# Orders of all engines with fewer changes between the matmul kinds of TensorE, and a gate transpose from a padded tile

## The chip, the cores and the metric

The kernel runs on one core of one Trainium2 chip. The metric is the device time of one execution in microseconds (us), lower is better.

## The reference

128 sequences (B) of S = 128 positions with D = 256 features, and a context of the same shape, go through four layers. All arithmetic is in float32.

```python
# layer 0, for every sequence; 16 heads of 16
z  = mha(x, x, Wq1, Wk1, Wv1, causal=True);  x1 = layernorm(x + z)
z  = mha(x1, ctx, Wq2, Wk2, Wv2);            x2 = layernorm(x1 + z)
x  = layernorm(x2 + relu(x2 @ fc1.T + b) @ fc2.T + b)
# inside mha: lengths = sum(energy[:, :, 0, :] != 0); key columns beyond the length get -inf
# layer 1: gate of width 4
nX, nF = layernorm(ctx), layernorm(x)
h  = gelu(attention(nF, nX, nX) @ fc1_w.T + fc1_b)      # 4 values a position
cr = h @ fc2_w.T + fc2_b;   nc = layernorm(cr)
x  = nF + gamma2 * (cr + gamma1 * attention(nc, nc, nc))
# layer 2
x  = x + softmax(x @ ctx.T) @ ctx
# layer 3: the mixer, 8 heads of 32, then a scan over the positions
y  = x + mha(layernorm(x), layernorm(ctx)) @ W_o.T + b_o
u  = (layernorm(y) @ W_in.T + b_in) @ Bmat
s_t = silu(s_{t-1} @ A.T) + u_t;   out = y + s @ Cmat + mod
```

## The kernel before

The sequences are worked on in 64 groups (g) of two (`G = 2`, line 25). The kernel has a prelude (weights, constants), a main phase over the groups, and a last phase for the scan over the 128 positions. The change is in the main phase.

**Software pipeline.** The work on a group is cut into some hundred steps per engine, each in one of ten units (`self_in`, `self_att`, `ctx_in`, `ctx_att`, `ffn`, `pair`, `real`, `mix_in`, `mix_att`, `mix_out`). `PROGRAM` (line 132) writes out by hand the order of steps on each engine. An entry such as `pair.yT@5` means: in round i, run step `yT` of unit `pair` for group i - 5. The number after the @ is the lag. `drive` (line 242) runs one order for rounds 0 to 69 and leaves out groups that don't exist; on SP the full rounds are a loop, on the other engines they are unrolled. Each step waits, by semaphores that count finished steps, for what it reads and for the buffer it writes (`Steps`, `Ring`). `BANKS` gives each product of TensorE one of eight PSUM banks; a bank is free when the step that read its last content is done. TensorE's 109 entries are the longest order in time.

**Steps of TensorE.** They differ in which part of the 128 x 128 array they use:
- over the whole array: `turned` (four transposes of 128 columns, L652), the transposes of probabilities `turn` (L730) and of outputs `back` (L777), projections (eight matmuls of 256 columns, L660 and L668), a bfloat16 causal tile of 512 columns (L679), and the pair steps (L831 to L909). A float32 matmul that is no transpose shows as two MATMUL records;
- in row strips: `scores.br` (L700) for sequence b and strip r, and `scores_mix` (L717), whose operands lie in 32 partitions each;
- in column strips: `values.br` (L764, the mixer's L759) and `e0` (L810), whose stationary operand has 32 columns and whose output is 32 partitions. A step of self and ctx values has one product in each of the four strips; a mixer's step r has its four products in two strips, `(DH * r + a) % 4 * 32`, the strips 0 and 1 for even r, 2 and 3 for odd r.

**The gate.** `gelu` writes four values a position into `y5`, whose fifth column is 1 (it carries the bias). `yT` transposes it on TensorE (L874), ScalarE copies five partitions of the result (L1051), and `cross` multiplies them by `w_cross` (L882):

```python
y5 = sb("y5", [128, G, 5])
last = nc.tensor.transpose(t[0:5, b * S:(b + 1) * S], y5[:, b, :], ident[:])
```

**The load of x.** `x` is held in one buffer. `load_self` (L594) waits until the group before has been transposed by TensorE (`xT`) and read by VectorE (`amax`, L1204):

```python
waits_apart(sp, prep, *latest(self_in["pe"].before("xT", g), self_in["dve"].before("amax", g)))
sp.dma_start(nat["X"][:], x_g[g]).then_inc(x_in.sem, 16)
```

**VectorE** takes the maxima of the scores (L1144), subtracts them (L1155), sums the mixer's rows (L1166) and does the statistics of the norms; **ScalarE** does exponentials (L978) and copies PSUM to SBUF (L968, L988, L1003); **GpSimd** does gains, biases and residual sums; **SP** issues all loads and stores.

## Time and profile before

| | |
|---|---|
| median of 3 runs | 4374.66 us (4370.78 to 4374.66) |
| the profiled execution's own time | 4371.99 us |
| its span, first to last instruction | 4370.2 us |
| instructions | 112146 |
| busy: TensorE, VectorE, ScalarE, GpSimd | 94%, 80%, 73%, 66% |
| granted TensorE clock, mean | 0.986 |

PE is TensorE's matmul, PEld its load of the stationary operand, which runs beside it; DVE is VectorE, ACT ScalarE, POOL GpSimd, SP the engine that issues DMAs. An engine's busy time counts overlapping instructions once. Matmuls are pipelined: one starts long before the end of the one before, so what a matmul costs in a stream is the distance between two starts and not its duration. A line of the timeline gathers equal neighbours (x8 is eight instructions).

### The profile page before, as it was taken

What the parts mean: (1) busy time and instruction counts of PE and PEld (TensorE: products, weight loads), DVE (VectorE), ACT (ScalarE), POOL (GpSimd) and SP (SyncE); (2) the same over time, 40 slices, a digit from 0 to 9 for tenths busy, and PEclk for the clock granted to TensorE, in tenths of its full rate; (3) what the DMA queues carried; (4) which work ended last, traced back from release to release, by engine and by line L of the source; (5) the groups of instructions that cost most, each with busy time, mean ns of one, the idle gap of its engine ahead of it and who ended that gap; (6) DMA issues with size and microseconds to landing.
All of it is one profiled execution on the core that took longest, in us unless ns stands there. A gap on an engine that the chain in (4) does not pass through costs nothing. (4 is left out here: it accounts for less than half of the span.)

```text
span 4370.2 us, 112146 instructions
## 1 busy us (share of the span) xinstructions
...
## 2 busy tenths in 40 slices
...
DMA packets 127586, 159.99 MB, mean 37 GB/s; under 512 B 23925, under 2 KB 114362, under 8 KB 122618
## 3 DMA queue, kind: packets, MB, share of 16 engines
...
q14 instruction: 242, 1.98, 0.2%
...
## 5 line engine op out<-in xcount | busy, mean ns | idle before, releaser
L988 ACT ACTIVATE probT<-bank 128x512 f32<-128x512 f32 x1280 | 741.4, 597 | 340.3 <-PE bank L730 337.0
L1144 DVE TENSOR_REDUCE mx<-bank 128x4 f32<-128x512 f32 x1280 | 834.4, 681 | 138.1 <-PE bank L700 104.2
L1155 DVE TENSOR_TENSOR prob<-bank,mx 128x512 f32<-128x512 f32 x1280 | 857.5, 683 | 40.1 <-PE bank L730 15.4
L978 ACT ACTIVATE prob<-prob 128x512 f32<-128x512 f32 x1280 | 783.5, 638 | 29.3 <-DVE prob L1155 28.0
L968 ACT ACTIVATE turned<-bank 128x512 f32<-128x512 f32 x896 | 531.8, 602 | 346.5 <-PE bank L652 192.7
L730 PE MATMUL bank<-ident,prob 128*128 128x128 f32 x5120 | 750.3, 280 | 31.8 <-POOL prob L1480 20.9
L730 PEld LDWEIGHTS bank<-ident,prob 128*128 128x128 f32 x5120 | 569.3, 142 | 126.9 <-issue 92.3
L660 PE MATMUL bank<-turned,shared 128*128 128x256 f32 x2560 | 606.0, 384 | 2.3 <-ACT turned L968 2.3
L660 PEld LDWEIGHTS bank<-turned,shared 128*128 128x128 f32 x2560 | 473.9, 191 | 81.7 <-issue 23.2
L1469 POOL TENSOR_SCALAR shared<-turned,half_of 128x512 f32<-128x512 f32 x256 | 397.9, 1565 | 200.7 <-ACT turned L968 200.7
L1390 POOL TENSOR_TENSOR rs_ln<-ve_ln,half 128x2 f32<-128x2 f32 x320 | 225.8, 705 | 333.1 <-DVE ve_ln L1133 333.1
L700 PE MATMUL bank<-shared,turned 32*128 32x256 f32 x4096 | 373.8, 403 | 11.4 <-POOL shared L1469 2.1
L668 PE MATMUL bank<-shared,turned 128*128 128x256 f32 x1536 | 369.9, 384 | 0.2 <-ACT probT L988 0.2
L1404 POOL TENSOR_TENSOR X<-X,row_ln_g 128x512 f32<-128x512 f32 x192 | 245.6, 1279 | 174.2 <-ACT X L1038 167.1
L1480 POOL TENSOR_TENSOR prob<-prob,inv 128x512 f32<-128x512 f32 x256 | 266.5, 1042 | 127.6 <-DVE inv L1171 127.6
L764 PE MATMUL bank<-probT,shared 128*32 128x128 f32 x8192 | 316.6, 278 | 9.1
L700 PEld LDWEIGHTS bank<-shared,turned 32*128 32x128 f32 x4096 | 264.2, 186 | 71.7 <-issue 65.7
L668 PEld LDWEIGHTS bank<-shared,turned 128*128 128x128 f32 x1536 | 277.0, 190 | 38.4 <-ACT probT L988 0.6
L764 PEld LDWEIGHTS bank<-probT,shared 128*32 128x32 f32 x8192 | 196.6, 109 | 119.1 <-issue 118.4
L1410 POOL TENSOR_TENSOR X<-X,row_ln_b 128x512 f32<-128x512 f32 x192 | 244.3, 1273 | 15.1
L844 PE MATMUL bank<-turned 128*128 128x128 f32 x1536 | 210.4, 280 | 3.0 <-ACT turned L968 2.9
L844 PEld LDWEIGHTS bank<-turned 128*128 128x128 f32 x1536 | 187.2, 192 | 11.7 <-ACT turned L968 4.1
...
## 6 DMA issues: line engine op xcount, KB each, us to landing
shared<-in_x SPq DMA_DIRECT2D x128, 256.0 KB, 3.5
CB<-in_ctx SPq DMA_DIRECT2D x64, 256.0 KB, 3.2
CC<-in_ctx SPq DMA_DIRECT2D x64, 256.0 KB, 2.7
mod<-mod_rows SPq DMA_DIRECT2D x64, 256.0 KB, 3.5
residual<-X SPq DMA_DIRECT2D x64, 256.0 KB, 2.2
...
```

Source lines behind the costliest of these rows:

```text
L660: last = nc.tensor.matmul(t[:, m * W:(m + 1) * W], w[:, a, m * 128:(m + 1) * 128], src[:, a, :], start=(a == 0), stop=(a == DH - 1))
L668: last = nc.tensor.matmul(t[:, b * D:(b + 1) * D], src[:, a, b * S:(b + 1) * S], w[:, a, :], start=(a == 0), stop=(a == DH - 1))
L700: last = nc.tensor.matmul(t[:, a * W:(a + 1) * W], QT[p][rows_, a, b * S:(b + 1) * S], KEYS[p][rows_, a, :, b * S:(b + 1) * S], start=(p ! ...
L730: last = nc.tensor.transpose(t[:, h * 128:(h + 1) * 128], src[:, h, :], ident[:])
L764: last = nc.tensor.matmul(t[k * 32:(k + 1) * 32, r * 128:(r + 1) * 128], VP[p][:, b, 4 * r + k, :], src[:, k, :], start=True, stop=True)
L844: last = nc.tensor.matmul(t[:, b * S:(b + 1) * S], qT[:, a, b * S:(b + 1) * S], kT[:, a, b * S:(b + 1) * S], start=(a == 0), stop=(a == DH ...
L968: nc.scalar.activation(dst, banks.of(f"{unit}.{name}")[:, 0:n], ACT.Copy).then_inc(*st["act"].mark(name))
L978: nc.scalar.activation(flat(t), flat(t), ACT.Exp, scale=SCALE[p]).then_inc(*st["act"].mark(f"exp.{b}{r}"))
L988: nc.scalar.activation(flat(t), banks.of(f"{att}.turn.{b}{r}")[:, :], ACT.Copy).then_inc(*st["act"].mark(f"probT.{b}{r}"))
L1144: nc.vector.tensor_reduce(m[:], banks.of(f"{att}.tile.{b}{r}")[:, :].rearrange("p (h t) -> p h t", h=4), AX, ALU.max)\
L1155: nc.vector.tensor_tensor(t[:], banks.of(f"{att}.tile.{b}{r}")[:, :].rearrange("p (h t) -> p h t", h=4), maxes.of(f"{att}.max.{b}{r}")[:]. ...
L1469: last = nc.gpsimd.tensor_scalar(KEYS[p][:, :, c, :], KT[p][:], half_of[:, c:c + 1], None, ALU.mult)
```

## The change

The orders of TensorE, ScalarE, VectorE, GpSimd and SP are written anew. The steps are the same, with some at another lag (`self_in.e0` at 1 and not 2, `self_in.amax` at 2 and not 1, `real.ccT` at 5 and not 4, `ctx_att.copies` at 3, `pair.load` at 4 and so on). TensorE's new order has longer runs of `values` and `scores` steps next to each other. All bank numbers are new. `y5` gets 128 columns for each sequence, all set to 1 in the prelude, and is transposed whole, into 128 partitions of the bank; ScalarE still copies five.

```diff
     "pe": """
-        self_in.e0@2 mix_att.scores.00@6 ctx_att.turn.10@4 ctx_att.values.00@4 ctx_att.values.01@4 ctx_att.turn.12@4
-        ctx_att.turn.11@4 pair.yT@5 ctx_att.values.03@4 ctx_att.turn.13@4 pair.cross@5 self_att.causal.02@2
-        ctx_att.values.02@4 ctx_att.values.12@4 self_att.causal.00@2 self_att.causal.03@2 ctx_att.values.10@4
-        ctx_in.x1T@3 self_att.causal.01@2 ctx_att.back.0@4 self_att.scores.01@2 self_att.scores.02@2
-        self_att.scores.00@2 self_att.scores.03@2 ctx_att.values.11@4 ctx_att.values.13@4 mix_att.turn.03@6
-        mix_in.k@5 ctx_att.back.1@4 mix_att.turn.02@6 ctx_in.q@3 pair.ncT@5 self_att.causal.10@2 mix_att.values.02@6
-        mix_att.values.03@6 mix_att.turn.00@6 self_in.len@2 pair.sc2@5 self_att.turn.01@2 mix_att.turn.01@6
-        self_att.causal.11@2 self_att.causal.12@2 mix_att.values.00@6 self_att.scores.10@2 self_att.scores.11@2
-        self_att.scores.12@2 pair.pT2@5 mix_att.values.01@6 ctx_in.cT@3 pair.av@5 mix_in.v@5 ffn.x2T@4 ctx_in.k@3
-        ffn.fc1@4 real.x4T@5 self_att.turn.03@2 ctx_in.e0@3 self_att.turn.00@2 real.screal@5 ffn.fc2@4 mix_out.o@6
-        real.pTreal@5 self_in.xT@1 self_att.turn.02@2 real.av@5 self_att.causal.13@2 self_att.scores.13@2
-        ctx_att.scores.02@3 ctx_att.scores.00@3 ctx_att.scores.03@3 ctx_att.scores.01@3 self_att.values.01@2
-        self_att.values.00@2 self_att.values.03@2 self_att.values.02@2 self_att.turn.10@2 ctx_in.v@3 self_in.q@1
-        ctx_in.len@3 self_att.turn.12@2 self_att.turn.11@2 self_att.turn.13@2 self_in.v@1 self_att.back.0@2
-        ctx_att.turn.00@3 ctx_att.turn.01@3 self_att.values.10@2 self_att.values.12@2 self_att.values.13@2
-        self_att.values.11@2 ctx_att.scores.10@3 ctx_att.scores.12@3 ctx_att.scores.13@3 ctx_att.scores.11@3
-        self_in.k@1 pair.CT@4 real.ccT@4 mix_out.h6T@6 pair.FT@4 self_att.back.1@2 ctx_att.turn.03@3 real.h5T@5
-        pair.sc1@4 ctx_att.turn.02@3 pair.vx@4 mix_in.q@5 pair.pT1@4 mix_out.u@6 pair.av1@4
+        mix_att.scores.00@6 ctx_att.turn.12@4 ctx_att.values.01@4 ctx_att.values.03@4 ctx_att.values.00@4
+        ctx_att.values.02@4 pair.yT@5 ctx_att.turn.10@4 ctx_att.turn.11@4 pair.cross@5 self_att.causal.02@2
+        ctx_in.x1T@3 real.ccT@5 ctx_att.turn.13@4 mix_in.k@5 ctx_att.back.0@4 self_att.causal.00@2
+        ctx_att.values.10@4 ctx_att.values.13@4 ctx_att.values.12@4 ctx_att.values.11@4 self_att.causal.03@2
+        self_att.causal.01@2 self_att.scores.01@2 self_att.scores.03@2 self_att.scores.02@2 self_att.scores.00@2
+        mix_att.turn.03@6 ctx_att.back.1@4 ctx_in.q@3 mix_att.turn.02@6 pair.ncT@5 self_in.len@2 mix_att.turn.00@6
+        self_in.xT@1 pair.sc2@5 self_att.causal.11@2 self_att.causal.10@2 self_att.causal.12@2 mix_att.turn.01@6
+        self_att.scores.10@2 self_att.scores.12@2 self_att.scores.11@2 mix_att.values.00@6 mix_att.values.02@6
+        mix_att.values.01@6 mix_att.values.03@6 pair.pT2@5 self_att.turn.01@2 ctx_in.cT@3 pair.av@5 mix_in.v@5
+        self_att.turn.00@2 ffn.x2T@4 ctx_in.k@3 ffn.fc1@4 real.x4T@5 ctx_in.e0@3 self_att.turn.03@2
+        self_att.causal.13@2 real.screal@5 ffn.fc2@4 mix_out.o@6 real.pTreal@5 self_att.turn.12@2 self_att.turn.02@2
+        real.av@5 ctx_in.len@3 self_att.scores.13@2 ctx_att.scores.03@3 ctx_att.scores.00@3 ctx_att.scores.01@3
+        ctx_att.scores.02@3 self_att.values.00@2 self_att.values.02@2 self_att.values.03@2 self_att.values.01@2
+        self_in.q@1 self_att.turn.11@2 self_att.turn.10@2 ctx_in.v@3 self_att.turn.13@2 self_att.back.0@2
+        self_in.v@1 ctx_att.turn.00@3 ctx_att.turn.01@3 self_att.values.12@2 self_att.values.13@2
+        self_att.values.10@2 self_att.values.11@2 ctx_att.scores.10@3 ctx_att.scores.13@3 ctx_att.scores.11@3
+        ctx_att.scores.12@3 pair.CT@4 self_in.k@1 mix_out.h6T@6 pair.FT@4 ctx_att.turn.03@3 real.h5T@5
+        self_att.back.1@2 pair.sc1@4 mix_in.q@5 ctx_att.turn.02@3 pair.vx@4 pair.pT1@4 mix_out.u@6 pair.av1@4
+        self_in.e0@1
     """,
...
     "dve": """
-        self_att.ln1ve@3 self_in.nz@2 self_in.count@2 mix_att.max.03@6 mix_att.max.00@6 mix_att.max.02@6
-        mix_att.centre.03@6 mix_att.centre.02@6 mix_att.max.01@6 mix_att.centre.00@6 mix_att.centre.01@6
-        mix_att.sum.03@6 self_in.spread@2 mix_att.recip.03@6 pair.lnNstats@5 pair.lnNaggr@5 ctx_in.amax@3
-        pair.lnNve@5 mix_att.sum.02@6 ctx_att.recip.0@4 mix_att.recip.02@6 ctx_att.norm.0@4 mix_att.sum.00@6
...
-        ctx_att.centre.10@3 ctx_att.centre.12@3 pair.NXT@4 self_in.amax@1 ctx_att.centre.11@3 ctx_att.max.13@3
...
+        mix_att.centre.03@6 mix_att.max.02@6 mix_att.max.01@6 mix_att.centre.02@6 mix_att.centre.01@6
+        mix_att.sum.03@6 mix_att.recip.03@6 pair.lnNstats@5 mix_att.centre.00@6 pair.lnNaggr@5 self_in.spread@2
+        pair.lnNve@5 mix_att.sum.02@6 ctx_att.recip.0@4 mix_att.recip.02@6 mix_att.sum.00@6 ctx_att.norm.0@4
+        mix_in.k@5 self_in.amax@2 mix_att.recip.00@6 self_att.max.01@2 mix_att.sum.01@6 ctx_att.recip.1@4
...
+        pair.a4@4 self_in.count@1 mix_att.max.03@5 mix_att.max.00@5
     """,
...
     "sp": """
-        mix_out.load@6 mix_out.store@6 mix_out.store_u@6 ctx_in.load@2 self_att.load@1 self_in.load@0 pair.load@3
+        pair.load@4 ctx_in.load@2 self_att.load@2 mix_out.load@5 mix_out.store@6 self_in.load@0 mix_out.store_u@6
     """,
...
-        y5 = sb("y5", [128, G, 5])
+        y5 = sb("y5", [128, G, 128])
...
-                        last = nc.tensor.transpose(t[0:5, b * S:(b + 1) * S], y5[:, b, :], ident[:])
+                        last = nc.tensor.transpose(t[:, b * S:(b + 1) * S], y5[:, b, :], ident[:])
```

## Rows read from the trace of the kernel before

**Rows 1.** Windows: stretch, length, busy PE, PEld, DVE, ACT, POOL, PE clock, DMA, GB/s.

```profile
249.00:3986.00 3737.00, 3699.43 (x34368) 3044.37 (x34548) 3173.46 (x8726) 2931.84 (x6162) 2644.68 (x2928) 1.00 0.09 28
```

**Rows 2.** Line 874, the gate's transpose: duration min/median/max ns, first and last start.

```profile
L874 PE MATMUL bank<-ident,y x128: 272/273/275, 249.0 to 4163.1; 128*5 128x128 f32 x128
```

**Rows 3.** Waits, PE's costliest, 1000 to 3000 us: us in total, times, longest.

```profile
PE bank L717 <- DVE mv_ln L1126: 0.8, 2, 0.5
```

**Rows 4.** Timeline, PE, 2052 to 2057: start us, length us, line, count.

```profile
2052.36 1.17 PE L717 MATMUL bank<-keys,turned 32*128 32x128 f32 x32
2053.46 0.66 PE L730 MATMUL bank<-ident,prob 128*128 128x128 f32 x4
2054.05 0.64 PE L764 MATMUL bank<-probT,shared 128*32 128x128 f32 x16
2054.62 1.09 PE L730 MATMUL bank<-ident,prob 128*128 128x128 f32 x8
2055.61 0.38 PE L874 MATMUL bank<-ident,y 128*5 128x128 f32 x2
2055.93 0.42 PE L764 MATMUL bank<-probT,shared 128*32 128x128 f32 x8
2056.28 0.66 PE L730 MATMUL bank<-ident,prob 128*128 128x128 f32 x4
2056.78 1.03 PE L882 MATMUL bank<-w_cross,y5T 128*128 128x256 f32 x4
```

**Rows 5.** Timeline, PE, 2021 to 2045.

```profile
2021.64 1.89 PE L668 MATMUL bank<-shared,turned 128*128 128x256 f32 x8
2023.37 1.89 PE L668 MATMUL bank<-w_o,turned 128*128 128x256 f32 x8
...
2040.02 1.29 PE L700 MATMUL bank<-shared,turned 32*128 32x256 f32 x16
2041.25 1.99 PE L660 MATMUL bank<-turned,shared 128*128 128x256 f32 x8
2043.08 0.60 PE L652 MATMUL bank<-ident,HC 128*128 128x128 f32 x4
2043.52 0.60 PE L652 MATMUL bank<-ident,CC 128*128 128x128 f32 x4
2044.12 0.66 PE L652 MATMUL bank<-ident,H 128*128 128x128 f32 x4
```

**Rows 6.** Timeline, PE, 2005 to 2010, with the mixer's values (L759).

```profile
2005.74 0.66 PE L759 MATMUL bank<-probT,vp 128*32 128x128 f32 x16
2006.33 0.66 PE L730 MATMUL bank<-ident,prob 128*128 128x128 f32 x4
...
2009.33 0.63 PE L759 MATMUL bank<-probT,vp 128*32 128x128 f32 x8
2009.89 1.15 PE L700 MATMUL bank<-shared,turned 32*128 32x256 f32 x12
```

**Rows 7.** Groups by form, 1000 to 3000 us: busy us, mean ns, idle before.

```profile
L730 PEld LDWEIGHTS bank<-ident,prob 128*128 128x128 f32 x2564 | 282.9, 141 | 46.0 <-issue 31.7 <-ACT probT L988 6.2 <-DVE mx L1144 0.4
...
L874 PEld LDWEIGHTS bank<-ident,y 128*5 128x5 f32 x64 | 3.0, 85 | 5.2 <-ACT probT L988 1.5
```

**Rows 8.** Timeline, SP: issues of loads, start us, length us.

```profile
2053.76 0.37 SPq L600 DMA_DIRECT2D shared<-in_x  x1
2054.50 1.57 SPq L594 DMA_DIRECT2D shared<-in_x  x1
```

**Rows 9.** Timeline, DVE, 2053 to 2063.

```profile
2053.66 1.89 DVE L1144 TENSOR_REDUCE mx<-bank 128x4 f32<-128x512 f32 x3 [0.49 <-PE bank L717]
...
2062.42 0.68 DVE L1166 TENSOR_REDUCE den<-prob 128x4 f32<-128x512 f32 x1
```

**Rows 10.** DMA issues, KB each, us to landing: 2020 to 2045, then 1990 to 2120.

```profile
CC<-in_ctx SPq DMA_DIRECT2D x1, 256.0 KB, 3.8
...
shared<-in_x SPq DMA_DIRECT2D x6, 256.0 KB, 4.3
```

More of the change, by code:

```diff
@@ L177 @@
-        self_att.centre.10@2 pair.sa@5 self_att.max.12@2 self_att.max.11@2 self_in.keep@2 ctx_in.q0@3 self_in.vp@2
-        ffn.relu@4 ctx_in.nz@3 self_att.centre.11@2 real.mxreal@5 real.nmreal@5 self_att.centre.12@2 ffn.sum@4
-        real.rsreal@5 ffn.ln3stats@4 ffn.ln3aggr@4 ffn.ln3ve@4 ctx_in.count@3 mix_out.res@6 mix_out.ln6stats@6
-        real.x5@5 ctx_att.max.00@3 ctx_att.max.01@3 self_att.max.13@2 real.ln5stats@5 ctx_att.centre.00@3
-        mix_out.ln6aggr@6 ctx_in.spread@3 self_att.centre.13@2 pair.lnFstats@4 pair.lnFaggr@4 ctx_att.max.03@3
@@ new lines @@
+        self_att.centre.01@2 ctx_att.norm.1@4 self_att.max.00@2 self_att.max.02@2 mix_att.recip.01@6
+        self_att.centre.00@2 ctx_att.ln2stats@4 self_in.valid@2 ctx_att.ln2aggr@4 pair.mx2@5 ctx_att.ln2ve@4
+        self_in.keep@2 pair.nm2@5 ctx_in.amax@3 ctx_in.keep@3 self_att.max.03@2 self_att.centre.03@2
+        self_att.centre.02@2 pair.rs2@5 self_att.max.11@2 self_att.max.12@2 pair.sa@5 self_att.centre.12@2
+        self_att.max.10@2 ctx_in.q0@3 self_att.centre.11@2 self_in.vp@2 ffn.relu@4 self_att.centre.10@2 ctx_in.nz@3
@@ new lines @@
+        ctx_in.count@3 real.mxreal@5 real.nmreal@5 ffn.sum@4 ctx_in.spread@3 ffn.ln3stats@4 real.rsreal@5
+        ffn.ln3aggr@4 ffn.ln3ve@4 mix_out.res@6 mix_out.ln6stats@6 mix_out.ln6aggr@6 ctx_in.valid@3 mix_out.ln6ve@6
+        real.x5@5 self_att.max.13@2 ctx_att.max.00@3 ctx_att.max.01@3 ctx_att.centre.00@3 self_att.centre.13@2
+        real.ln5stats@5 pair.lnFstats@4 ctx_att.centre.01@3 pair.lnFaggr@4 pair.lnFve@4 real.ln5aggr@5
+        pair.lnCstats@4 ctx_att.max.02@3 pair.lnCaggr@4 self_att.recip.0@2 real.ln5ve@5 self_in.q0@1 pair.lnCve@4
@@ L188 @@
     """,
     "pool": """
-        self_att.add@3 real.x5b@6 ctx_att.copies@4 self_att.ln1pow@3 ffn.copies@4 self_att.ln1nmr@3 ffn.biased@4
-        self_att.keep@3 self_att.ln1gain@3 self_att.ln1@3 mix_att.part.03@6 pair.lnNpow@5 pair.lnNnmr@5
-        mix_att.part.02@6 pair.lnNgain@5 pair.lnN@5 mix_att.part.00@6 ctx_att.add@4 mix_att.part.01@6
-        ctx_att.ln2pow@4 ctx_att.ln2nmr@4 ctx_in.mask@3 ctx_att.ln2gain@4 ctx_att.ln2@4 pair.skip@5 pair.gam2@5
-        pair.x4@5 ctx_in.keys@3 ffn.x2b@4 ffn.ln3pow@4 ffn.ln3nmr@4 ffn.ln3gain@4 ffn.ln3@4 pair.lnFpow@4
@@ L195 @@
-        mix_out.ln6pow@6 pair.lnFnmr@4 mix_out.ln6nmr@6 pair.lnCpow@4 pair.lnCnmr@4 pair.lnFgain@4 real.ln5pow@5
-        real.ln5nmr@5 pair.lnF@4 mix_out.mod@6 self_in.keys@1
+        self_in.keys@2 mix_att.part.03@6 pair.lnNpow@5 pair.lnNnmr@5 mix_att.part.02@6 pair.lnNgain@5 pair.lnN@5
+        mix_att.part.00@6 ctx_att.add@4 mix_att.part.01@6 ctx_att.ln2pow@4 ctx_att.ln2nmr@4 ctx_in.mask@3
+        ctx_att.ln2gain@4 ctx_att.ln2@4 pair.skip@5 pair.gam2@5 pair.x4@5 ffn.x2b@4 ctx_in.keys@3 ffn.ln3pow@4
@@ L209 @@
-    ctx_att.tile.01:0 ctx_att.tile.02:7 ctx_att.tile.03:4 ctx_att.turn.00:2 ctx_att.turn.01:1 ctx_att.turn.02:5
-    ctx_att.turn.03:0 ctx_att.back.0:6 ctx_att.tile.10:0 ctx_att.tile.11:1 ctx_att.tile.12:6 ctx_att.tile.13:3
-    ctx_att.turn.10:4 ctx_att.turn.11:2 ctx_att.turn.12:5 ctx_att.turn.13:5 ctx_att.back.1:4 ffn.x2T:1 ffn.fc1:6
-    ffn.fc2:0 pair.CT:7 pair.FT:4 pair.vx:4 pair.sc1:2 pair.pT1:5 pair.av1:3 pair.yT:4 pair.cross:4 pair.ncT:1
-    pair.sc2:1 pair.pT2:1 pair.av:1 real.x4T:1 real.ccT:2 real.screal:1 real.pTreal:5 real.av:2 real.h5T:7
```

64 lines of the change are left out of this document (34 added, 30 removed).

## Prediction

> **What bounds the kernel now.** I read first which engine is busiest, and where. The table by windows says that from 249 to 3986 us TensorE is busy 3699 of 3737 us at a granted clock of 1.00, VectorE 3173, ScalarE 2932, GpSimd 2645 [rows 1]. The gate's transpose, once in each round of the pipeline, first runs at 249.0 and last at 4163.1 us, 64 rounds [rows 2]; 3914 us over 63 intervals is 62.1 us a round, and near 62.4 in the full stretch. The waits say who is late there: in 2000 us TensorE waits 0.8 us in its costliest group [rows 3]; the idle time of the others is theirs to spend. So TensorE's own order sets the pace. A microsecond taken from one round is taken from about 63: some 60 rounds are full (3737 / 62.4), and I count the partly filled ones at both ends as 3 more.
>
> A busy TensorE is not one at its peak, so the next view is its timeline, read by the starts of neighbouring lines. The steps come in three kinds: over the whole array (F), in column strips (C: values, e0), in row strips (R: scores). The difference of two starts shows a price wherever the kind changes:
> - Without a change, a step of four transposes takes 0.44 us (2043.08 to 2043.52), 0.11 for each; a projection of eight records 1.73 (2021.64 to 2023.37), so 0.22 for 256 columns, and as much for a causal tile; a C step of eight records 0.22, since 16 of them take 0.57 and 8 take 0.35 [rows 4, 5].
> - F to C: the two transposes at 2055.61 take 0.32 in place of 0.22, so 0.10 is lost. Within the stay, 16 matmuls take 0.57 in place of 0.44, 0.13 lost. Back in F, the four at 2056.28 take 0.50, 0.06 lost. One stay in C costs 0.29 us; I book 0.14 on entering C and 0.15 on returning to F [rows 4].
> - A projection after R takes 1.83 in place of 1.73 [rows 5].
>
> **The change, part by part.**
> *Orders.* Going once round each order, with the wrap, gives 29 changes of kind before and 20 after. Runs of C go from 12 to 7, of R from 5 to 5, of F from 12 to 8. Of the returns to F, one before and one after begins with a causal tile and one with a projection; these cancel. The others begin with transposes: ten before, six after. So 5 x 0.14 + 4 x 0.15 = 1.30 us a round go. One R run that followed C now follows F; I take both entries as equal, the nearest rows being 0.10 for F to C and 0.12 for C to R (2009.33 to 2009.89 is 0.56 for what takes 0.44 in itself) [rows 4, 6].
>
> *The mixer's values.* A step of these uses two of the four strips for four turns of 0.11 us. Before, steps 02 and 03, of unlike strips, took 0.59 together, and a single step 0.56 [rows 6]; 00 and 01 stood alone. Less 0.13 for each of three stays that is 1.32 us. After, one stay holds 00, 02, 01, 03. If nothing overlaps, 4 x 0.44 = 1.76; if both pairs do, 0.88. Only the middle pair are neighbours of unlike strips, so I take the middle, 1.32: no change, with -0.44 and +0.44 as ends.
>
> *The padded gate tile.* The transpose now loads 128 columns, not 5: 141 ns and not 85 [rows 7]. Transposes start every 0.11 us whichever they load, so it is hidden; uncovered twice a round it would be 0.1 us. It now follows a C run directly, and the return to F is counted above. The one memset of the larger tile stands outside the loop. Zero.
>
> *Moved waits.* VectorE, ScalarE and GpSimd keep their instructions, with 9.4, 13 and 18 us free in a round [rows 1]. ScalarE and GpSimd are given new places, but what TensorE needs of them keeps a microsecond or so of other matmuls between, as before: I take zero, and the rival on waits holds the rest. One distance shrinks much. The load of x for a round waits until VectorE's amax has read the last one (single buffer). amax moves from the end of VectorE's order to its first fifth (@1 to @2), TensorE's transpose of x from the middle to the first third, both now in the same round. Before, x is issued at 2054.50 [rows 8] and is wanted a half round later. After: VectorE's first maximum starts 1.30 us after the mixer's scores start (2053.66 against 2052.36), and the same sequence up to its third sum ends 9.4 us on, at 2063.1 [rows 4, 9]. It loses one reduction and gains the keys and amax, +0.6: amax ends 11.4 us after the scores. TensorE, from the same start to the transpose of x: 1.10 for the scores, 12 x 0.44 for transposes, 0.22 for the gate's, 0.87 cross, 2 x 1.73, 4 x 0.22 causal, 0.1 length, 8 x 0.22 values, 1.23 for a run of scores with its way out, 0.29 for each of two stays in C and 0.2 for the other changes: 15.7 us. That leaves 4.3 us less some 0.1 for semaphores, 4.2, for a load. Lone and crowded loads land in 3.8 and 4.3 us [rows 10], and SP takes up to 0.7 us from one issue to the next [rows 8], so 3.8 to 5.0 are needed: a stall of 0 to 0.8 us a round. I take 0.2, what the middle of both gives (4.4). SP's other loads are then issued behind it or behind real.av, with half a round or more before their use: zero. Behind a late x TensorE's whole order queues, from a quarter of the round on; next in it are the gate's second scores and the self tiles, for which VectorE and ScalarE wait.
>
> *Sum.* 1.30 - 0.20 = 1.10 us a round, x 63 = 69 us. The profiled execution took 4371.99 us, 1.8 over its span and 2.7 under the median 4374.66: 4303 in its terms, **4305 us** in the median's, 1.6% less.
>
> A rule to weigh: the rows show 0.10 us lost on entering C and 0.15 in all on returning [rows 4]. The Trainium skill (TensorEngine Tiling (Array Packing), Tiling Modes) says that a change of tiling mode drains the TensorE, which this agrees with. Its page TensorE: Matmul & The Clock Gate (Single matmul latency, Back-to-back issue gap) prices an isolated warm matmul at (398+N)/2.4 ns against N/2.4 + 2.5 in a stream; an estimate from that page is 163 ns a drain, 9 x 0.163 x 63 = 92 us in place of 82, and 4295 us in all. The trace's prices hold in the sum.
>
> **The rivals.**
> - *Half given back.* x comes 0.5 to 1.2 us late, or new waits of that size stand at other tight places. For it: 4.2 us against 3.8 to 5.0. Against: where TensorE itself lags in the steps before, the gap is wider. 0.1 to 0.8 us a round remain: 4324 to 4368. Chance 0.20.
> - *Slower.* The same place, with the long issue: one of SP's loads of x shows 1.57 us of issue where others show 0.37 [rows 8]. Then 4.3 + 0.7 + 1.2 = 6.2 against 4.2, 2.0 late, 0.7 more than is won: +44 us, 4419. It decides from 1.3 us late on. Against: it needs every worst end in every round. Chance 0.09.
> - *More.* TensorE's old order has small gaps that no change of kind explains, from 0.06 (eight transposes at 2054.62 take 0.99, not 0.93) to 0.16 (four at 2043.52 take 0.60, not 0.44) [rows 4, 5]; I count eight, with what follows them 0.8 us a round. If the new orders close them and x is in time: 2.1 x 63 = 132 us, 4242. Chance 0.10.
> - *It doesn't do what it says.* A change of kind costs only because a wait falls there, and the waits move along: no change. Against: the same 0.29 stands at every stay I read. Chance 0.04.
>
> **How the numbers follow.** The forecast, 4285 to 4325, has 0.57. The range must leave out 0.2: it reaches down halfway to the fourth case and up over most of the second, **4255 to 4352**. 0.2% (9 us) is about what a measurement here can tell from no change. Faster 0.57 + 0.20 + 0.10 = 0.87, within 0.2% 0.04, slower 0.09.
>
> **What would show it.** The gate's transpose at intervals near 61.3 us. Stays of 16 or 32 values in C at 0.57 and 1.01; TensorE's matmul count unchanged. Changes of kind that still lose 0.10, 0.13 and 0.06. The start of the transpose of X against the one before: 0.44 if x is in time, more if not; and the issue of x 11.5 us after the mixer's scores. I am wrong if the stays cost the same but the round does not shrink (then look for a new wait, first at X), if the mixer's four values take other than 1.45 with their exit, or if VectorE no longer waits for TensorE.

## The result and the profile after

The kernel after takes 4246.34 us, median of 4 runs (4244.74 to 4250.19), beside 4372.95 us of the kernel before on the same chip (4370.78 to 4374.66): a ratio of 0.9712, 95% interval 0.9695 to 0.9729. The forecast was 4305 us in 4255 to 4352. The direction was right, the gain came out at 126.6 us where 69 were forecast, and the time fell below the range.

First the page of the kernel after (span; busy us, share, instructions):

```profile
span 4245.0 us, 112221 instructions
...
PE 4043.7 (95%) x37547; PEld 3385.5 (80%) x37547; DVE 3430.2 (81%) x9517; ACT 3171.7 (75%) x6721; POOL 2911.0 (69%) x3172
```

and its full stretch by windows, with the columns of [rows 1]:

```profile
244.00:3866.00 3622.00, 3612.38 (x34470) 3064.27 (x34470) 3120.79 (x8710) 2912.86 (x6141) 2657.71 (x2926) 1.00 0.10 29
```

TensorE still sets the pace, at the same granted clock of 1.00, and is busy for 3612 of 3622 us, 99.7%. The 99.0% of [rows 1] is no lower share: that trace lacks the records of three causal tiles in each round, and early_mod_load, a kernel below with the same round and all its records, shows 3725.57 of 3737 us in the same stretch, 99.7% too. The gate's transpose answers to [rows 2]:

```profile
L875 PE MATMUL bank<-ident,y x128: 272/286/332, 243.9 to 4048.5; 128*128 128x128 f32 x128
```

It splits the 125.2 us that left the span. Between the first and the last transpose lie 3804.6 us where [rows 2] have 3914.1: 109.5 us, 60.4 a round and not 62.1 (60.6 in the full stretch; I forecast 61.3). Ahead of the first lie 5.1 us less. Behind the last lie 196.5 us, before 207.1: 10.6 less.

The timeline of PE at the mixer's values, which answers to [rows 6], and from the mixer's scores on, which answers to [rows 4] (start us, length us; source lines count one higher after the change):

```profile
2010.36 0.63 PE L731 MATMUL bank<-ident,prob 128*128 128x128 f32 x4
2010.82 0.60 PE L653 MATMUL bank<-ident,shared 128*128 128x128 f32 x4
...
2014.41 1.54 PE L760 MATMUL bank<-probT,vp 128*32 128x128 f32 x32
2015.88 0.44 PE L858 MATMUL bank<-ident,pc 128*128 128x128 f32 x2
...
2055.77 1.17 PE L718 MATMUL bank<-keys,turned 32*128 32x128 f32 x32
2056.87 0.66 PE L731 MATMUL bank<-ident,prob 128*128 128x128 f32 x4
2057.46 1.08 PE L765 MATMUL bank<-probT,shared 128*32 128x128 f32 x32
2058.47 0.44 PE L875 MATMUL bank<-ident,y 128*128 128x128 f32 x2
...
2062.13 1.89 PE L661 MATMUL bank<-turned,w_k 128*128 128x256 f32 x8
```

Three of the prediction's terms can be read at once. A stay of 32 values takes 1.01 us from start to start (2057.46 to 2058.47), as said. The mixer's four values take 1.47 (2014.41 to 2015.88), forecast 1.45: their term is zero. The transpose of x (L653, `shared`) starts 0.46 us behind the one before it, forecast 0.44 if x is in time: no stall there. The stretch from the mixer's scores to `mix_in.k` (L661, `w_k`) is 6.36 us, with a different set of steps in it.

### The profile page after: what moved, and what is told of

Its sections match the earlier page's. It is cut to its first block, busy times and chain, and to the rows that moved or that the text cites. A ratio compares the mean times of both kernels' runs of the same rounds, so it can differ in the third digit from the quotient of the medians.

```text
span 4245.0 us, 112221 instructions
## 1 busy us (share of the span) xinstructions
PE 4043.7 (95%) x37547; PEld 3385.5 (80%) x37547; DVE 3430.2 (81%) x9517; ACT 3171.7 (75%) x6721; POOL 2911.0 (69%) x3172
## 4 chain that ended last, share of the span: by engine, by line
PE 68%; ACT 12%; POOL 7%; issue 5%; DVE 3%; DMA 0%; ACTq 0%; DVEq 0%; POOLq 0%; SPq 0%
PE bank L661 15%; PE bank L731 9%; PE bank L653 7%; PE bank L669 6%; PE bank L845 4%; PE bank L701 3%; PE bank L765 3%; ACT prob L979 3%; PE bank L680 3%; PE bank L760 2%; POOL rs_ln L1391 2%; PE bank L778 2%; POOL X L1411 2%; POOL X L1405 2%; ACT probT L989 2%
## 5 line engine op out<-in xcount | busy, mean ns | idle before, releaser
L1156 DVE TENSOR_TENSOR prob<-bank,mx 128x512 f32<-128x512 f32 x1280 | 847.8, 679 | 55.5 <-PE bank L731 34.0
L989 ACT ACTIVATE probT<-bank 128x512 f32<-128x512 f32 x1280 | 753.2, 600 | 160.3 <-PE bank L765 101.4
L979 ACT ACTIVATE prob<-prob 128x512 f32<-128x512 f32 x1280 | 795.4, 641 | 21.7 <-DVE prob L1156 20.6
L731 PEld LDWEIGHTS bank<-ident,prob 128*128 128x128 f32 x5120 | 592.3, 142 | 126.1 <-issue 38.1
L661 PE MATMUL bank<-turned,shared 128*128 128x256 f32 x2560 | 605.4, 384 | 1.8 <-ACT turned L969 1.8
L661 PEld LDWEIGHTS bank<-turned,shared 128*128 128x128 f32 x2560 | 468.3, 191 | 69.9 <-issue 14.3
L701 PE MATMUL bank<-shared,turned 32*128 32x256 f32 x4096 | 364.4, 402 | 2.7 <-POOL shared L1470 2.7
L701 PEld LDWEIGHTS bank<-shared,turned 32*128 32x128 f32 x4096 | 251.1, 186 | 77.3 <-issue 68.2
L765 PE MATMUL bank<-probT,shared 128*32 128x128 f32 x8192 | 277.1, 276 | 2.5 <-DVE nz_self L1228 2.5
L765 PEld LDWEIGHTS bank<-probT,shared 128*32 128x32 f32 x8192 | 208.2, 109 | 65.6 <-issue 61.9
L1454 POOL TENSOR_TENSOR Z<-Z,shared 128x512 f32<-128x512 f32 x64 | 81.6, 1275 | 185.8 <-DVE Z L1195 185.8
```

Of the source, the lines that this page charges most:

```text
L661: last = nc.tensor.matmul(t[:, m * W:(m + 1) * W], w[:, a, m * 128:(m + 1) * 128], src[:, a, :], start=(a == 0), stop=(a == DH - 1))
L701: last = nc.tensor.matmul(t[:, a * W:(a + 1) * W], QT[p][rows_, a, b * S:(b + 1) * S], KEYS[p][rows_, a, :, b * S:(b + 1) * S], start=(p ! ...
L731: last = nc.tensor.transpose(t[:, h * 128:(h + 1) * 128], src[:, h, :], ident[:])
L765: last = nc.tensor.matmul(t[k * 32:(k + 1) * 32, r * 128:(r + 1) * 128], VP[p][:, b, 4 * r + k, :], src[:, k, :], start=True, stop=True)
L979: nc.scalar.activation(flat(t), flat(t), ACT.Exp, scale=SCALE[p]).then_inc(*st["act"].mark(f"exp.{b}{r}"))
L989: nc.scalar.activation(flat(t), banks.of(f"{att}.turn.{b}{r}")[:, :], ACT.Copy).then_inc(*st["act"].mark(f"probT.{b}{r}"))
```

## The experiments

Twelve kernels beside the two. "Round" is the distance from the first to the last gate transpose over 63; "behind" is the time from the last one to the end of the span.

| kernel | changes of kind | us | before on that chip | ratio, 95% interval | round | behind |
|---|---|---|---|---|---|---|
| before | 29 | | | | 62.1 | 207.1 |
| after | 20 | 4246.34 | 4372.95 | 0.9712, 0.9695 to 0.9729 | 60.4 | 196.5 |
| pad_only | 29 | 4376.85 | 4372.68 | 1.0010, 1.0001 to 1.0019 | 62.2 | 207.5 |
| split_stays | 28 | 4313.86 | 4372.68 | 0.9870, 0.9855 to 0.9885 | 61.5 | 195.9 |
| regroup_before | 23 | 4358.06 | 4372.68 | 0.9967, 0.9954 to 0.9980 | 61.9 | 207.5 |
| banks_before | 29 | 4361.38 | 4372.68 | 0.9975, 0.9966 to 0.9984 | 61.9 | 210.4 |
| early_mod_load | 29 | 4363.33 | 4375.73 | 0.9973, 0.9963 to 0.9983 | 62.1 | 197.0 |
| merge_mixer | 27 | 4355.47 | 4375.73 | 0.9956, 0.9943 to 0.9970 | 61.8 | 206.9 |
| regroup_and_scalar | 23 | 4418.10 | 4375.73 | 1.0098, 1.0083 to 1.0113 | 62.9 | 207.1 |
| banks_after | 20 | 4250.14 | 4375.73 | 0.9715, 0.9702 to 0.9728 | 60.4 | 196.7 |
| ln1_back | 20 | 4332.41 | 4373.57 | 0.9907, 0.9892 to 0.9922 | 61.7 | 195.3 |
| x_later | 20 | 4318.72 | 4373.57 | 0.9876, 0.9860 to 0.9891 | 61.4 | 196.3 |
| best1 | 20 | 4238.34 | 4373.57 | 0.9693, 0.9680 to 0.9706 | 60.2 | 196.4 |
| best2 | 20 | 4270.03 | 4372.81 | 0.9764, 0.9750 to 0.9777 | 60.7 | 195.5 |

### The padded tile by itself

The kernel before with

```diff
-        y5 = sb("y5", [128, G, 5])
+        y5 = sb("y5", [128, G, 128])
-                        last = nc.tensor.transpose(t[0:5, b * S:(b + 1) * S], y5[:, b, :], ident[:])
+                        last = nc.tensor.transpose(t[:, b * S:(b + 1) * S], y5[:, b, :], ident[:])
```

> The kernel before with the one edit to the gate's values: a tile of 128 columns, turned whole. My theory: the four matmuls of the step stay whole-array matmuls, two in each direction of the same stream, and only one copy waits behind them, so 0 us (-4 to +4), and the gate's transpose lasts as long as in the kernel before. Rival, the five-column tile was a change of kind of its own, entered and left at 0.14 us each: up to 0.29 us in each of 64 rounds, -18 us.

4.2 us above the kernel before, a ratio of 1.0010 (1.0001 to 1.0019): at most 0.2% lost, and no gain. The tile of 5 columns was no kind of its own. By the starts of the steps, the distance from the gate's transpose to the values behind it grew from 0.31 to 0.37 us, some 3 us over the rounds, so in the kernel before the longer load is not quite hidden. The padding brings nothing; the gain must come from the orders and banks.

### The price of a change of kind, first read backwards

The kernel after, four of its runs of values cut again:

```diff
-  ctx_att.back.0@4 self_att.causal.00@2 ctx_att.values.10@4 ctx_att.values.13@4 ctx_att.values.12@4
-  ctx_att.values.11@4 self_att.causal.03@2
+  ctx_att.back.0@4 ctx_att.values.10@4 self_att.causal.00@2 ctx_att.values.13@4 self_att.causal.03@2
+  ctx_att.values.12@4 ctx_att.values.11@4
-  mix_att.values.03@6 pair.pT2@5 self_att.turn.01@2
+  self_att.turn.01@2 mix_att.values.03@6 pair.pT2@5
-  ctx_att.turn.01@3 self_att.values.12@2 self_att.values.13@2 self_att.values.10@2
+  self_att.values.12@2 self_att.values.13@2 ctx_att.turn.01@3 self_att.values.10@2
```

> The kernel after, with four of its runs of values cut again: one transpose or mask matmul that was a neighbour of the run is put into its middle, so the round has 28 changes of kind where it has 20. Nothing else moves, and each of the four steps put inside is moved by under 0.9 us and has its data and its bank by then (the tightest by 0.35 us). Theory 1, the time is in the changes of kind, at 0.14 to 0.15 us each: 8 x 0.145 x 64 = +74 us against the kernel after (60 to 85), 60.6 us a round become 61.8. Theory 2, the gain came from waits that the new order and new banks closed, and changes of kind hide behind the queues of the four strips: under 15 us. Against the kernel before, theory 1 gives about -53 us, theory 2 about -115.

67.5 us above the kernel after (4313.86 against 4246.34), with chips whose kernel before differs by 0.3: 67.5 / (8 x 64) = 0.132 us for a change. Its timeline of PE at the twice cut run of values:

```profile
2035.53 0.43 PE L764 MATMUL bank<-probT,shared 128*32 128x128 f32 x8
2035.89 0.39 PE L679 MATMUL bank<-causal,ident_b 128*128 128x512 bf16 x1
2036.21 0.42 PE L764 MATMUL bank<-probT,shared 128*32 128x128 f32 x8
2036.57 0.39 PE L679 MATMUL bank<-causal,ident_b 128*128 128x512 bf16 x1
2036.89 0.64 PE L764 MATMUL bank<-probT,shared 128*32 128x128 f32 x16
```

A step of values takes 0.36 us where it takes 0.22 in a run, and a causal tile 0.32 where it takes 0.22: 0.14 and 0.10 lost. Added up over the steps at the four places, the eight changes cost 1.05 us a round, 0.132 each. Theory 1 holds, a little under its price of 74. That the whole round agrees so well is partly luck: with `turn.01` gone from behind pT2, the second gate product (`av`) waits for ScalarE's copy of pT2 (`pct`), which the expectation did not see (us in total in 1000 to 3000 us, times, longest),

```profile
PEld bank L893 <- ACT pct L968: 11.3, 33, 0.6
```

and costs 0.36 us a round, while small waits elsewhere shrink by 0.30. Time ahead of the first and behind the last gate transpose stays as in the kernel after.

### The same change forwards: no clean price, and two stays that bring nothing

The kernel before, TensorE's order alone:

```diff
-  ctx_att.values.00@4 ctx_att.values.01@4 ctx_att.turn.12@4 ctx_att.turn.11@4 pair.yT@5 ctx_att.values.03@4
+  ctx_att.values.00@4 ctx_att.values.01@4 ctx_att.values.03@4 ctx_att.turn.12@4 ctx_att.turn.11@4 pair.yT@5
-  ctx_att.values.12@4 self_att.causal.00@2 self_att.causal.03@2 ctx_att.values.10@4
+  ctx_att.values.12@4 ctx_att.values.10@4 self_att.causal.00@2 self_att.causal.03@2
-  mix_att.values.00@6 self_att.scores.10@2 self_att.scores.11@2 self_att.scores.12@2 pair.pT2@5 mix_att.values.01@6
+  self_att.scores.10@2 self_att.scores.11@2 self_att.scores.12@2 mix_att.values.00@6 mix_att.values.01@6 pair.pT2@5
```

> The kernel before, with TensorE's order alone changed and the other engines' orders, the banks and the lags as they were: three of its short stays among the values are joined to a neighbour, so 23 changes of kind where there are 29. Theory 1, 0.145 us each: 6 x 0.145 x 64 = -56 us (-40 to -65). Theory 2, the gain needs the other engines' orders and the banks: within 15 us of the kernel before. Fill and drain: if their 15.6 us came from TensorE's order too, the first gate transpose and the stretch behind the last one move here as well; I expect them within 3 us of the kernel before.

14.6 us, a quarter of theory 1's 56: my expectation fell. So I took the third edit alone:

> The kernel before with one short stay among the values removed instead of three: the mixer's values.00 and values.01 joined behind the R run, 27 changes of kind. From the run with all three removed (-14.6 us) the rounds' steps showed the two stays of the context's values given back within 10 us of the round, and this one kept. If so: -0.25 x 64 = -16 us (-12 to -19), as much as the three together. If instead each stay gave a third, -5.

20.3 us: this one stay brings all that the three bring together and more. It is no clean price of a change of kind, though 20.3 / (2 x 64) = 0.16 looks like one, for the edit does two things more. In the kernel before, values.00 stood alone as in [rows 6], and values.01 too:

```profile
2011.34 0.63 PE L759 MATMUL bank<-probT,vp 128*32 128x128 f32 x8
2011.90 0.66 PE L652 MATMUL bank<-ident,CB 128*128 128x128 f32 x4
```

In merge_mixer they are neighbours:

```profile
2063.94 0.66 PE L759 MATMUL bank<-probT,vp 128*32 128x128 f32 x16
2064.53 0.44 PE L857 MATMUL bank<-ident,pc 128*128 128x128 f32 x2
2064.81 0.60 PE L652 MATMUL bank<-ident,CB 128*128 128x128 f32 x4
2065.50 1.13 PE L893 MATMUL bank<-NC,pct 128*128 128x256 f32 x4
```

The two steps take 0.56 us each alone and 0.59 together, because 00 and 01 use unlike strips and overlap, as 02 and 03 do in [rows 6]. That saves 0.53 us, and the lead-in ahead of the stay 0.09; by the lone step's 0.56 less 0.13, I estimate that some 0.4 of these 0.63 is the overlap and some 0.2 the two changes of kind. Against it, pT2 now stands right ahead of C's transpose, and `av` starts 0.69 us behind that transpose and not 0.49: it waits for the copy of pT2 (11.3 us in 33 waits, as in split_stays), and 0.31 us a round is given back. Net 0.32, just above what was expected, and made up of other terms. What a change of kind costs is therefore shown backwards alone.

The two context stays bring nothing. The timeline of PE in the kernel with three stays removed shows it:

```profile
2045.37 1.17 PE L717 MATMUL bank<-keys,turned 32*128 32x128 f32 x32
...
2050.90 0.86 PE L764 MATMUL bank<-probT,shared 128*32 128x128 f32 x24
2051.69 0.75 PE L679 MATMUL bank<-causal,ident_b 128*128 128x512 bf16 x2
2052.54 0.66 PE L652 MATMUL bank<-ident,X 128*128 128x128 f32 x4
...
2055.95 1.89 PE L660 MATMUL bank<-turned,w_k 128*128 128x256 f32 x8
```

From the mixer's scores to `w_k` it takes 10.58 us with two stays fewer; the kernel before takes 10.61 for the same steps (2052.36 in [rows 4] to its `w_k` at 2062.97). The two causal tiles behind the values now take 0.85 to the next start (2051.69 to 2052.54), where two take 0.44 and the return from C 0.10: the second waits until ScalarE has copied out of its bank, and x1T behind it for the bank of `cross`. Both wait for ScalarE, whose timeline in that stretch is full:

```profile
2045.51 1.28 ACT L1046 ACT_TABLE_LOAD   x1
2046.81 0.21 ACT L1046 ACTIVATE y<-a 128x8 f32<-128x8 f32 x1
2047.00 1.09 ACT L1038 ACTIVATE X<-Z,nmr_ln,rs_ln 128x256 f32<-128x256 f32 x2
2047.99 1.14 ACT L988 ACTIVATE probT<-bank 128x512 f32<-128x512 f32 x2
2049.20 0.37 ACT L1051 ACTIVATE y5T<-bank 5x256 f32<-5x256 f32 x1
2049.59 1.28 ACT L978 ACT_TABLE_LOAD   x1
2050.88 0.63 ACT L978 ACTIVATE prob<-prob 128x512 f32<-128x512 f32 x1
```

Twice 1.28 us of it load a table of functions, for the gelu and back for the exponential. No other instruction of ScalarE runs beside them.

### ScalarE's place in that stretch

The kernel with three stays removed, ScalarE's step `self_att.ln1` moved:

```diff
-  pair.gelu@5 self_att.ln1@3 ctx_att.probT.10@4 ctx_att.probT.12@4 pair.yT@5 mix_att.exp.03@6
+  pair.gelu@5 ctx_att.probT.10@4 ctx_att.probT.12@4 pair.yT@5 self_att.ln1@3 mix_att.exp.03@6
```

> The kernel with three stays removed, and in ScalarE's order one step moved: self_att.ln1, 0.59 us, goes from ahead of the probT.10, probT.12 and yT copies to behind them. Theory: in that stretch ScalarE runs back to back for 9 us (from ln1 to the copy of outT.1), and TensorE's gain from the two context stays turned into waits for its copies; with the copies 0.5 us earlier the gain of both comes through: a further -0.4 to -0.58 us a round, -26 to -37 us, about -45 against the kernel before. Rival, another engine's chain (the gelu behind the second gate product) sets the stretch: within 5 us of the kernel with three stays removed (-14.6).

It became slower, 42 us above the kernel before and 57 above the one it was made from. The fix was wrong, and the trace shows why and that the place was right:

```profile
2012.50 0.21 ACT L1046 ACTIVATE y<-a 128x8 f32<-128x8 f32 x1
2013.45 0.60 ACT L988 ACTIVATE probT<-bank 128x512 f32<-128x512 f32 x1 [0.74 <-PE bank L764]
...
2015.16 1.08 ACT L1038 ACTIVATE X<-Z,nmr_ln,rs_ln 128x256 f32<-128x256 f32 x2
2016.26 1.28 ACT L978 ACT_TABLE_LOAD   x1
```

With ln1 gone from ahead of it, the first copy does not start sooner: it waits 0.74 us for the values that release its buffer. ln1 had filled that wait; now it stands in front of the table load. From the gelu to the exponential's end it is 5.69 us, before the move 4.70 (2046.81 to 2051.51): 0.99 later, and a round is 1.0 us longer (62.9 against 61.9). By the starts of TensorE's steps all of it stands at one place, a causal tile whose bank ScalarE must first copy (probT):

```profile
PEld bank L679 <- ACT probT L988: 40.0, 32, 1.3
```

40.0 us in 32 waits, where the kernel with three stays removed has 8.3. A microsecond put into ScalarE's queue here is a microsecond of the round, so ScalarE sets this stretch once the two context stays are gone from it, and this is why they brought nothing.

The other direction, in the kernel after, whose ScalarE runs ln1 ahead of the gelu:

```diff
-  ctx_att.exp.13@4 self_att.ln1@3 pair.gelu@5 ctx_att.probT.12@4
+  ctx_att.exp.13@4 pair.gelu@5 self_att.ln1@3 ctx_att.probT.12@4
```

> The kernel after with one step of ScalarE's order put where the kernel before has it: self_att.ln1 (0.59 us) behind the gelu, not ahead of it. Theory: behind the mixer's scores the kernels are held by ScalarE's queue, from the gelu to the copy of NC's transpose, and the kernel after got its unforecast gain there because this step left the queue and now runs ahead of the gelu, in time in which ScalarE waits anyway. Then its place costs +0.45 to +0.6 us a round, +28 to +38 us against the kernel after. Rival, the stretch is TensorE's own time and its fewer changes of kind: within 5 us.

86 us above the kernel after, over twice what was expected. The waits of PE (what waits for whom, us in 1000 to 3000, times, longest):

```profile
PE bank L730 <- ACT probT L988: 20.3, 32, 1.0
```

0.63 us a round in this one wait, for the copy of probT.12. I had priced only this. By the distances of TensorE's steps, round 1.40 us longer, 0.74 are at this wait, 0.32 at the transpose of x1T and 0.35 at ctx_att.back.1: x1T's data come through GpSimd (two steps of 1.3 us behind ln1), which I had left out, and GpSimd's shift makes ScalarE's own lnN late, ahead of outT.1 (read from the timelines; no run moves the two apart). The theory of ScalarE's queue holds; its price was too small by what hangs on ln1 elsewhere. That this place is worth more than the whole unforecast gain also says that it is a condition of the short stretch and no term of a sum.

### Banks alone

The kernel before, orders untouched:

```diff
-  self_in.e0:2 mix_att.tile.01:6 ctx_att.turn.11:2 self_att.tile.01:3 ctx_att.back.0:6
+  self_in.e0:5 mix_att.tile.01:2 ctx_att.turn.11:6 self_att.tile.01:6 ctx_att.back.0:3
-  pair.ncT:1 mix_att.turn.00:3 self_in.v:3 mix_out.h6T:5 pair.FT:4
+  pair.ncT:3 mix_att.turn.00:4 self_in.v:6 mix_out.h6T:4 pair.FT:5
-  real.h5T:7 pair.sc1:2 pair.vx:4 mix_in.q:1 mix_out.u:0
+  real.h5T:2 pair.sc1:7 pair.vx:1 mix_in.q:4 mix_out.u:6
```

> The kernel before, its orders untouched, with 15 of the 89 bank assignments changed so that four steps that stood behind a bank still being read have one that is free: the H6 transpose, self_in.v, causal.03 and the mixer's scores. 29 changes of kind as before. Theory A, my forecast was short because the new banks and orders close small bank waits: these four cost 0.23, 0.15, 0.15 and 0.1 us a round by their excess over the usual distance, so about -0.55 x 64 = -35 us (-20 to -45). Theory B, a closed wait returns at the next step that waits for its data: under 10 us.

> The kernel after, orders untouched, with 19 of 89 bank assignments changed: C's transpose, the context's turn.10, back.0, self_in.len and a few more get banks that are free by then. Their excess over the usual distance is 0.17, 0.11, 0.03 and 0.06 us a round, with 0.06 of the mixer's turn.00. In the kernel before, 15 such changes gave a third of the sum of what they closed (11 of 35 us). By the full sum -27 us against the kernel after, by the third -9; I take -9 to -18, which would be faster than both kernels.

In the kernel before 11.3 us: a third of theory A's 35, and just over theory B's 10. By the distances of the steps, 0.18 us are saved at the mixer's scores and 0.15 are left at x1T, but 0.01 at the second pair scores, which wait for the copy of NC's transpose in both kernels; the 0.25 saved up to h6T, with no such wait behind it, stays. In the kernel after nothing, where 9 to 18 us were expected (ratio 0.9715 against 0.9712): the 0.11 us saved at turn.10 are gone at `cross`, the 0.18 at C's transpose at the first pair scores. In these two kernels, closing a bank wait ahead of a data wait brought nothing. (The change itself keeps six of its 89 bank numbers: not all are new.)

### Behind the last round

```diff
-        mix_out.load@6 mix_out.store@6 mix_out.store_u@6 ctx_in.load@2 self_att.load@1 self_in.load@0 pair.load@3
+        mix_out.load@5 mix_out.store@6 mix_out.store_u@6 ctx_in.load@2 self_att.load@1 self_in.load@0 pair.load@3
```

> The kernel before with the load of the modulation rows one lag earlier in SP's order, as the change has it; nothing else. Theory: the 10.5 us that the change saved behind the last gate transpose are this load. In the kernel before it is issued at 4163.50, right behind the scan's first big transfers, holds SP's queue for 32.93 us, and GpSimd waits 22.61 us for it at 4222.20, with the mixer's probabilities behind it. One lag earlier it is issued ahead of them: -9 to -11 us, all of it behind the last gate transpose, rounds as before. Rival, the drain is shorter for the fewer changes of kind and the other engines' orders: within 2 us of the kernel before.

12.4 us by the medians; behind the last gate transpose 197.0 us in place of 207.1, which is 10.1 less, in the kernel after 196.5. The rounds stay as they were. SP's timeline in the kernel before (start us, length us):

```profile
4162.59 0.86 SPq L587 DMA_DIRECT2D turned<-residual  x2
4163.50 32.93 SPq L615 DMA_DIRECT2D mod<-mod_rows  x1
```

and GpSimd's, which waits for these rows with the mixer's probabilities queued behind:

```profile
4222.20 1.26 POOL L1503 TENSOR_TENSOR X<-X,mod 128x512 f32<-128x512 f32 x1 [22.61 <-DMA mod<-mod_rows]
```

With the early load SP's is

```profile
4152.82 0.34 SPq L615 DMA_DIRECT2D mod<-mod_rows  x1
```

and GpSimd's

```profile
4199.04 1.27 POOL L1503 TENSOR_TENSOR X<-X,mod 128x512 f32<-128x512 f32 x1 [0.44 <-ACT H L1038]
```

Issued behind the scan's big transfers, the load held SP for 33 us; ahead of them, 0.34.

### The margin of x

The kernel after, on VectorE:

```diff
-  mix_in.k@5 self_in.amax@2 mix_att.recip.00@6 self_att.max.01@2 mix_att.sum.01@6 ctx_att.recip.1@4
+  mix_in.k@5 mix_att.recip.00@6 self_att.max.01@2 mix_att.sum.01@6 ctx_att.recip.1@4 self_in.amax@2
```

> The kernel after with DVE's amax step, which frees x's buffer, moved behind four steps (up to ctx_att.recip.1), so it ends 1.7 us later. In the kernel after it ends 4.0 us before TensorE has come to the transpose of the next x. My prediction took 3.8 to 5.0 us for issue and transfer, and priced the loss at 0.2 us a round; the trace shows the x load alone on the rings and landed after some 2.9 us. By that, 1.1 us are spare, and the later amax costs 1.74 - 1.1 = 0.6 us a round, +40 us against the kernel after (+25 to +55). By the 3.8 us of the prediction it would be 1.5 us a round, +97. If the transposes' place has more cover than I see, 0.

72.4 us above the kernel after, more than the 25 to 55 expected, at the transpose of x:

```profile
2046.92 0.63 PE L730 MATMUL bank<-ident,prob 128*128 128x128 f32 x4
2048.55 0.63 PE L652 MATMUL bank<-ident,shared 128*128 128x128 f32 x4 [1.00 <-DMA shared<-in_x]
```

It starts 1.63 us behind its neighbour where 0.46 is in time: 1.17 late in this round, 1.15 a round in the middle of the run. (Of the 72.4 us some 4 stand ahead of the first gate transpose, at 248.1 us and not 243.9.) amax ended 2.3 us later, not the 1.7 that I expected (the step's own length came on top), so 2.3 - 1.15 = 1.15 us were spare: the theory's 1.1, with its delay corrected.

### Towards a faster kernel

```diff
-  (ScalarE) ctx_att.outT.0@4 pair.yT@5 ... real.ccT@5 pair.lnN@5 mix_att.exp.01@6 ctx_att.outT.1@4 mix_att.probT.03@6
+  (ScalarE) pair.yT@5 ctx_att.outT.0@4 ... pair.lnN@5 mix_att.exp.01@6 ctx_att.outT.1@4 mix_att.probT.03@6 real.ccT@5
-  (TensorE) mix_att.turn.02@6 pair.ncT@5 ... pair.sc1@4 mix_in.q@5 ctx_att.turn.02@3
+  (TensorE) pair.ncT@5 mix_att.turn.02@6 ... ctx_att.turn.02@3 pair.sc1@4 mix_in.q@5
```

> An attempt at a faster kernel than the one after: ScalarE copies the gate's transpose ahead of outT.0 and CC's transpose behind the mixer's probT.03, where it idles 1.6 us; TensorE turns NC one step earlier and the context's turn.02 ahead of the first pair scores, which wait for F's copy; 24 banks changed to suit. Changes of kind as in the kernel after. The waits it aims at cost 0.145 (pair scores), 0.145 (mix_in.q), 0.11 (turn.10) and about 0.2 us a round (cross, mix_in.k, sc2). If the waits do not simply come back, -0.3 us a round, -20 us against the kernel after (4225); if the chain of small steps from F's copy to the second pair scores sets the time whatever stands between them, within 5 us. I give them even chances.

4238.34 us (0.9693 beside 0.9712 of the kernel after): 8 us less, short of the 20 hoped for, and the two intervals overlap, so that it is faster than the kernel after is not shown. It is the lowest time of the study. Its steps gained 0.43 us from the C transposes on and lost 0.37 at `mix_in.k`, so I went after that one.

```diff
-  (TensorE) ctx_att.turn.13@4 mix_in.k@5 ... ctx_att.values.13@4 ctx_att.values.12@4 ctx_att.values.11@4
+  (TensorE) mix_in.k@5 ctx_att.turn.13@4 ... ctx_att.values.12@4 ctx_att.values.11@4 ctx_att.values.13@4
-  (ScalarE) ctx_att.probT.13@4 mix_att.exp.00@6 ctx_in.x1T@3 pair.lnN@5 mix_att.exp.01@6 ctx_att.outT.1@4
+  (ScalarE) ctx_in.x1T@3 ctx_att.probT.13@4 mix_att.exp.00@6 ctx_att.outT.1@4 pair.lnN@5 mix_att.exp.01@6
```

> A second step from best1, whose trace shows the one large wait left behind the mixer's scores: mix_in.k stands for cross's copy in bank 5 and gives 0.37 us of the round back, while all eight banks are held. Here TensorE makes mix_in.k ahead of the context's turn.13, in the bank of the mixer's tile.01, which is free by then; ScalarE copies x1T ahead of probT.13 and outT.1 ahead of lnN, so that the transposes behind have their data; values.13 goes last in its run; 11 banks follow. If the wait was a bank's and nothing else: -0.3 to -0.37 us a round, -20 us against best1, about 4218. If NC's chain over GpSimd (lnN, its transpose, sc2) sets the stretch anyway, the wait moves there: within 5 us of best1, 4238.

31.7 us slower than best1. The waits of PE in 1000 to 3000 us:

```profile
PE bank L678 <- ACT probT L987: 11.5, 33, 0.4
PE bank L651 <- POOL NC L1409: 5.2, 32, 0.2
```

The wait of `mix_in.k` is closed (0.37 us), but the next mask tile (L678) waits in its place, and NC's transpose (L651) for GpSimd, 0.5 us behind best1 from there on. Neither theory met this: the wait moved on, as the second said, but two places wait where one did, and the round grew, which neither had forecast.

## Why the prediction was wrong

**The price of a kind and the count: right.** Nine changes at 0.14 to 0.15 were 1.30 us a round; read backwards one costs 0.132 (split_stays), 1.19 a round. 1.19 to 1.30 x 63 = 75 to 82 us. Forwards no run gives the price by itself. The Trainium skill's price for an isolated matmul (TensorE: Matmul & The Clock Gate, Single matmul latency), from which I estimated 0.163 us a change, is above what split_stays shows.

**The mixer's values and the padded tile: right,** zero each (1.47 us against 1.45; pad_only).

**The load of x: a mis-sized term.** I booked 0.2 us a round from a window of 4.2 us and a need of 3.8 to 5.0. x_later shows 1.15 us spare in the kernel after. The window was right: in the kernel after amax starts at

```profile
2066.41 0.68 DVE L1205 TENSOR_REDUCE amax_self<-shared 128x2 f32<-128x512 f32 x1
```

and so ends 11.3 us after the mixer's scores start (forecast 11.4), and TensorE comes to x 15.6 us after them (forecast 15.7), 4.3 later. The need was too large: x_later, which does wait, starts the transpose 3.1 us behind the end of amax. The 3.8 us that I took for a lone load [rows 10] was no lone one: SP issued the next load 0.94 us behind it (2027.39 and 2028.33). The DMA issues of 2006.5 to 2012 us in the kernel after (KB, us to landing) show this load nearly alone:

```profile
shared<-in_x SPq DMA_DIRECT2D x1, 256.0 KB, 2.7
```

and 2.6 to 3.1 us in two other rounds. The term should have been 0: 12.6 us of the miss. The rivals that lived on a late x ("half given back", "slower") went with it.

**"I take zero" for all other waits: the step that failed most.** By the distances of TensorE's steps over the full rounds, each against the shortest of its like (four transposes behind four transposes 0.44, and so on), the kernel before loses 1.17 us a round in waits and the kernel after 0.70: 0.47 us, 30 us in all. The profile's own waits say nearly the same, and said it before the change. "In 2000 us TensorE waits 0.8 us in its costliest group" is true of the matmuls alone [rows 3]: the waits for other engines stand on the load of the stationary operand ahead of them, PEld, of which [rows 7] show one group (6.2 us for ScalarE's probT). In 1000 to 3000 us of the kernel before the costliest are

```profile
PEld bank L679 <- ACT probT L988: 8.5, 32, 0.3
PEld bank L652 <- ACT turned L968: 7.8, 32, 0.2
PEld bank L652 <- ACT CR L968: 6.4, 32, 0.2
PEld bank L730 <- ACT probT L988: 6.2, 31, 0.2
```

and of the kernel after

```profile
PEld bank L653 <- ACT outT L1004: 16.6, 33, 0.8
PEld bank L718 <- ACT prob L979: 6.5, 33, 0.2
```

With the smaller groups that is 37.0 us in 32 rounds before and 24.0 in 33 after, 1.15 and 0.73 us a round (a load's wait need not delay its matmul by as much, so this gives the size and no exact price).

Together 1.30 + 0.47 = 1.77 us x 63 = 111, and 109.5 were measured. The rival "more" had this mechanism with 0.10 and 0.8 us a round; I had counted gaps in two stretches only, and gave small odds to an order written anew over all engines closing any.

Why they closed is shown only in part. ScalarE's place explains why the 1.30 us arrived, and not where the 0.47 came from: with the two context stays gone TensorE follows ScalarE's queue from the gelu on (they bring nothing, 1 us more in the queue costs 1.0), and in the kernel after ln1 runs ahead of the gelu (putting it back costs 86 us). But from the mixer's scores to NC's transpose the waits shrank by only some 0.1 us a round. More of them stood elsewhere in the kernel before: 0.18 us at the mixer's scores, 0.23 at H6's transpose and 0.15 at self_in.v, all for a bank, since banks_before closes these three by bank numbers alone and keeps 0.25 us a round. The kernel after has none of the three, and a new wait of 0.17 at the first pair scores. Which order or bank closed the others was not tried, nor was all of ScalarE's order moved into the kernel before.

**The ends: left out.** "I count the partly filled ones at both ends as 3 more" prices them like rounds. Behind the last gate transpose 10.6 us went, and early_mod_load shows 10.1 of them in one edit: `mix_out.load` at lag 5, ahead of the scan's transfers. I passed it by under "SP's other loads ... half a round or more before their use: zero", which holds in a full round and not in the last. 5.1 us went ahead of the first transpose. They hang on small things: with 19 other bank numbers and the change's orders (banks_after) the first transpose is at 250.6 us, in the kernel after at 243.9, before at 249.0. What there gives the 5 us stays open.

The sum in the end: 69 forecast + 12.6 (x) + 30 (waits) + 15.7 (ends) = 127 us, 126.6 measured. The 30 is what the same rounds leave over the shortest distances, so that the sum closes is no proof of its terms.
